# Statistics of the first two images from a separate 128-partition copy, and weights prepared in groups of three

## The reference

```python
xd = jnp.concatenate([x[:, :, 0::2, 0::2], x[:, :, 0::2, 1::2], x[:, :, 1::2, 0::2], x[:, :, 1::2, 1::2]], axis=1)
feats = jnp.concatenate([_dwconv(xd, w1, 1), _dwconv(xd, w3, 3), _dwconv(xd, w5, 5)], axis=1)
y = jnp.einsum('bchw,oc->bohw', feats, w_proj[:, :, 0, 0])
...
x = x + _L0_conv_ref(_gn(x), L0_conv_w1, L0_conv_w3, L0_conv_w5, L0_conv_w_proj)
```

## Time and profile before

| | us |
|---|---|
| median of three runs | 147.66 |
| lowest and highest | 146.65, 147.93 |
| the profiled execution | 147.7 |
| its span in the profile | 145.9 |
| TensorE busy (matmuls) | 129.1 |
| DVE busy | 119.8 |
| ACT busy | 103.0 |
| POOL busy | 98.3 |

### The profile page before, as it was taken

One profiled execution on the slowest core, in us unless ns is written; L12 is line 12 of the kernel. 1 busy time (PEld: TensorE's weight loads), 2 busy tenths in 40 slices (PEclk: granted clock), 3 DMA queues, 4 the chain that ended last, 5 costly groups with the idle time before them and its releaser, 6 DMA issues.

```text
span 145.9 us, 1480 instructions
## 1 busy us (share of the span) xinstructions
PE 129.1 (88%) x501; PEld 95.9 (66%) x501; DVE 119.8 (82%) x134; ACT 103.0 (71%) x110; POOL 98.3 (67%) x73
## 2 busy tenths in 40 slices
PE   0374699999999999999999999999999999999910
PEld 0222578788876777678767776777677867776600
DVE  0198999996299999999999999799938995999460
ACT  2285999999955999599959995999599950004100
POOL 7104799999699628994999399829993999100840
PEclk9999879999999999999999999999999999999996
DMA  3999993052043007000708699107094992853966
GB/s 101 216 210 212 209 211 50 0 110 49 0 98 57 0 19 136 0 4 17 136 0 180 122 186 206 38 17 136 0 216 84 174 198 55 180 112 85 196 145 150
DMA packets 35431, 15.73 MB, mean 108 GB/s; under 512 B 34016, under 2 KB 34144, under 8 KB 35040
## 3 DMA queue, kind: packets, MB, share of 16 engines
q1 hardware_dynamic: 33408, 8.39, 31.6%
q0 software_dynamic: 1440, 7.04, 24.9%
q10 hardware_dynamic: 576, 0.21, 0.6%
HBM read 4.41 MB, written 4.19 MB: 59 GB/s over the span
## 4 chain that ended last, share of the span: by engine, by line
PE 85%; DVE 4%; DMA 3%; ACT 2%; ACTq 1%; issue 1%; DVEq 1%; POOL 0%; POOLq 0%
PE YP L551 75%; PE YP L594 9%; DMA w_sb<-in_L_conv_w_dram 3%; DVE st L424 2%; DVE X L522 1%; ACT G L340 1%; DVE weff L449 1%; DVEq L86 0%; ACT HI L384 0%; PE SMALL L533 0%; POOL rstd L253 0%; ACTq L312 0%; ACTq L311 0%; PE SMALL L539 0%; ACTq L310 0%
## 5 line engine op out<-in xcount | busy, mean ns | idle before, releaser
L275 POOL TENSOR_TENSOR RING_SUM<-RING_SUM,PROD 128x900 f32<-128x900 f32 (+1 forms) x37 | 75.2, 2034 | 7.7 <-ACT PROD L365 3.8
L489 DVE SCALAR_TENSOR_TENSOR ACC<-G,coef,ACC 128x930 f32<-128x930 f32 (+1 forms) x64 | 76.6, 1197 | 2.0
L551 PE MATMUL YP<-HI,whi 128*128 128x512 f32 (+1 forms) x150 | 39.1, 413 | 2.8 <-ACT HI L384 2.8
L551 PE MATMUL YP<-LO,whi 128*128 128x512 f32 (+1 forms) x150 | 40.4, 420 | 0.0
L551 PE MATMUL YP<-HI,wlo 128*128 128x512 f32 (+1 forms) x150 | 37.7, 402 | 0.0
L551 PEld LDWEIGHTS YP<-HI,whi 128*128 128x128 f32 x150 | 29.5, 197 | 11.0 <-DVE whi L468 3.4
L365 ACT ACTIVATE PROD<-G,coef 128x900 f32<-128x900 f32 (+1 forms) x37 | 36.2, 1053 | 0.0
L551 PEld LDWEIGHTS YP<-LO,whi 128*128 128x128 f32 x150 | 28.5, 190 | 10.0 <-issue 3.4
L551 PEld LDWEIGHTS YP<-HI,wlo 128*128 128x128 f32 x150 | 28.3, 190 | 7.1
L375 ACT ACTIVATE Y<-YP 64x1024 f32<-64x1024 f32 x14 | 15.3, 1096 | 24.1 <-PE YP L594 23.9
L340 ACT ACTIVATE G<-X,nbias,rstd 64x1024 f32<-64x1024 f32 (+2 forms) x18 | 21.9, 1215 | 1.9 <-DVE nbias L442 1.5
(11 more groups left out here) (55 smaller groups left out, 50.3 us busy)
## 6 DMA issues: line engine op xcount, KB each, us to landing
LO<-G POOLq DMA_DIRECT2D x7, 543.0 KB, 4.9
X<-in_x_dram SPq DMA_DIRECT2D x12, 256.0 KB, 5.4
X<-Y POOLq DMA_DIRECT2D x3, 1024.0 KB, 7.0
out_dram<-X SPq DMA_DIRECT2D x12, 256.0 KB, 5.8
X<-in_x_dram SPq DMA_DIRECT2D x8, 128.0 KB, 4.3
out_dram<-X SPq DMA_DIRECT2D x8, 128.0 KB, 2.5
wp_sb<-in_L_conv_w_proj_dram ACTq DMA_DIRECT2D x1, 192.0 KB, 3.4
w_sb<-in_L_conv_w_dram ACTq DMA_DIRECT2D x1, 12.5 KB, 3.8
```

The lines of the kernel that those rows point to most:

```text
L275: pool.tensor_tensor(dst, dst, prod(b, k), ALU.add).then_inc(prod_added, 1)
L489: dve.scalar_tensor_tensor(part(ACC, tap), g_tap(b, tap), of5(tap), part(ACC, tap), ALU.mult, ALU.add).then_inc(acc_step, 1)
L551: mm = nc.tensor.matmul(dst, w[:, n, :], src, start=start, stop=False, skip_group_check=True)
```

## The change

- Images 0 and 1 get their statistics one by one. `load_parts` loads a second copy of each over all 128 partitions (a channel in four partitions, `XS`): image 0 in two DMAs ahead of everything else on SP's queue, image 1 behind image 0's normal load and w1. `part_bn` takes two statistics per image, spreads them with a mask, and a matmul with `same` (`sum_parts`) gives every partition the four parts of its channel; `part_variance` and `part_bias` finish it.
- The statistics of pairs 1 to 3 are as before but one place further on in `between`; `bn(1)` moves from ahead of the first tap into it.
- HI of image 0 is written straight from X: ACT writes three of four pieces (`high_half`), DVE one. G of image 0 is written after that, in one piece per column parity, and LO of image 0 as before from G and HI.
- The inner taps' weights come in three groups of three. ACT scales taps 0 to 4 and casts group 0; tap 5 is scaled behind ACT's first `high_half`; POOL scales taps 6 to 8. DVE casts groups 1 and 2. POOL subtracts group by group. The centre tap, which alone needs w1, becomes the last.
- The extra taps' scaling and cast move on ACT behind `products(0)`, and their `wlo` on POOL behind `sum_ring(0)`.
- w1 has its own load (SP's queue) and its own matmul. TensorE's `keep_warm` matmuls become 9 of 128 columns ahead of the transposes, 3 behind them, and 6 of 512 columns of zeros ahead of image 0.

```diff
-INNER = [(0, 0)] + [(dy, dx) for dy in (-1, 0, 1) for dx in (-1, 0, 1) if (dy, dx) != (0, 0)]
+INNER = [(0, -1), (0, 1)] + [(dy, dx) for dy in (-1, 1) for dx in (-1, 0, 1)] + [(0, 0)]
...
-WARM = (2, 2)
+WARM = (9, 3, 6)
+CHUNK = 3
+CHUNKS = N_INNER // CHUNK
+ACT_SCALED = 6
...
+            load_parts(sp, 0, 0, 512, xs_loaded[0])
+            load_parts(sp, 0, 512, 1024, xs_loaded[1])
+            load_image(sp, 0, image_loaded[0])
+            sp.dma_start(w_sb[:, W1_AT:N_COEF], w1.rearrange("c a h w -> c (a h w)")).then_inc(w1_loaded, 16)
+            load_parts(sp, 1, 0, 1024, xs_loaded[2])
+            load_image(sp, 1, image_loaded[1])
+            for b in range(2, B):
+                load_image(sp, b, x_loaded[b // 2])
...
+            pool.wait_ge(wpT_ready, 3)
+            pool.wait_ge(coef_copied, 1)
+            for n in range(ACT_SCALED, N_INNER):
+                pool.tensor_scalar(weff[:, n, :], wpT[:, 2, :], of5(PE_TAPS[n]), None, ALU.mult).then_inc(pool_scaled, 1)
             inv_std(1, 0, 1)
-
+            for k in range(CHUNKS):
+                taps = slice(k * CHUNK, (k + 1) * CHUNK)
+                pool.wait_ge(whi_ready, k + 1)
+                pool.tensor_tensor(wlo[:, taps, :], weff[:, taps, :],
+                                   whi[:, taps, :].bitcast(F32), ALU.subtract).then_inc(wlo_ready, 1)
+            inv_std(2, 1, 2)
+            sum_ring(0)
             pool.wait_ge(extra_ready, 1)
             pool.tensor_tensor(wlo[:, N_INNER:N_PE, :], weff[:, N_INNER:N_PE, :],
                                whi[:, N_INNER:N_PE, :].bitcast(F32), ALU.subtract).then_inc(extra_low_ready, 1)
-            pool.wait_ge(whi_ready, 1)
-            pool.tensor_tensor(wlo[:, 0:N_INNER, :], weff[:, 0:N_INNER, :],
-                               whi[:, 0:N_INNER, :].bitcast(F32), ALU.subtract).then_inc(wlo_ready, 1)
-            sum_ring(0)
-            inv_std(2, 1, 2)
+            inv_std(3, 2, 3)
...
             act.wait_ge(pads_zero, N_PADS)
+            act.wait_ge(image_loaded[0], 32)
             act.wait_ge(stats_ready, 1)
-
-            normalise(0, 0, TOP, g_top)
-            act.wait_ge(g_top, 2)
-            act.activation(s_image(HI, 0, 0, TOP), g_image(0, 0, TOP), ACT.Copy).then_inc(hi_top, 1)
-            normalise(0, TOP, PH, g_ready)
+            high_half(0, TOP, 0, hi_top)
+            scale_w5(5, ACT_SCALED)
+            high_half(TOP, PH, 0, hi_bottom)
+            high_half(TOP, PH, 1, hi_ready)
+            normalise(0, 0, PH, g_ready)
             act.wait_ge(g_ready, 2)
-            act.activation(s_image(HI, 0, TOP, PH), g_image(0, TOP, PH), ACT.Copy).then_inc(hi_ready, 1)
             products(0)
+            scale_w5(N_INNER, N_PE)
+            act.wait_ge(w5_scaled, ACT_SCALED + len(EXTRA))
+            act.activation(whi[:, N_INNER:N_PE, :], weff[:, N_INNER:N_PE, :], ACT.Copy).then_inc(extra_ready, 1)
...
+            def part_variance(b):
+
+                dve.wait_ge(spread_summed, b + 1)
+                dve.bn_aggr(agg1[:, b, :], SPREAD_PS[b]).then_inc(agg1_done, 1)
+                dve.wait_ge(agg1_done, b + 1)
+                dve.tensor_scalar(vare[:, b:b + 1], agg1[:, b, 1:2], EPS, None, ALU.add).then_inc(stat_step, 1)
...
-            between = {(0, 0): lambda: aggregate(1), (0, 2): lambda: (bn(2), aggregate(2)), (0, 3): lambda: variance(2, 1, 2),
...
+            between = {(0, 0): lambda: part_variance(1), (0, 1): lambda: (part_bias(1), bn(1)),
...
             for _ in range(WARM[1]):
-                keep_warm()
-            pe.wait_ge(whi_ready, 1)
+                keep_warm(ident[:, :], P)
+            pe.wait_ge(w_loaded, 32)
+            coefficients(0, W1_AT, coef_ready)
+            sum_parts(0)
```

More of the change, by code:

```diff
@@ L232, in _ @@
                                base=0, pattern=[[-1, P]], channel_multiplier=1).then_inc(const_step, 1)
+            pool.memset(same[:, :], 0.0).then_inc(stat_const, 1)
+            for k in range(PARTS):
+                pool.wait_ge(stat_const, k + 1)
+                v = same[:, :].rearrange("p (n c) -> p n c", c=C)
+                pool.affine_select(out=v, in_=v, compare_op=ALU.not_equal, fill=1.0, base=-k,
+                                   pattern=[[0, P // C], [-PARTS, C]], channel_multiplier=1).then_inc(stat_const, 1)
             a = avg[:, :].rearrange("p (b i c) -> p b i c", b=2, i=2)
@@ L319, in _ @@
                                ACT.Copy).then_inc(wpT_ready, 1)
+            act.wait_ge(coef_ready, 1)
+            act.activation(coef[:, 0:W1_AT], COEF_PS[:, 0:W1_AT], ACT.Copy).then_inc(coef_copied, 1)
             act.wait_ge(wpT_ready, 3)
@@ L326, in scale_w5, with high_half @@
                                    scale=of5(PE_TAPS[n])).then_inc(w5_scaled, 1)
-            scale_w5(0, N_PE)
-            act.wait_ge(w5_scaled, N_PE)
-            act.activation(whi[:, N_INNER:N_PE, :], weff[:, N_INNER:N_PE, :], ACT.Copy).then_inc(extra_ready, 1)
+            scale_w5(0, 5)
+            act.wait_ge(weff_step, CHUNK)
+            act.activation(whi[:, 0:CHUNK, :], weff[:, 0:CHUNK, :], ACT.Copy).then_inc(whi_ready, 1)
+            def high_half(r0, r1, j, done):
+                src = X[0:HALF, 0, r0:r1, :].rearrange("p h (w j) -> p h w j", j=2)[:, :, :, j]
+                act.activation(s_image(HI, 0, r0, r1)[HALF * j:HALF * (j + 1)], src, ACT.Identity,
+                               bias=nbias[0:HALF, 0:1], scale=rstd[0:HALF, 0:1]).then_inc(done, 1)
             def normalise(b, r0, r1, done):
@@ L452, in _ @@
+            part_bn(0)
             dve.wait_ge(wpT_ready, 3)
             dve.wait_ge(coef_copied, 1)
-            bn(0, 0, 2)
-            add_w3(0, 1, 2)
-            bn(0, 2, 4)
-            aggregate(0)
-            add_w3(3, 4)
-            variance(1, 0, 1)
-            add_w3(5, 6)
-            bias(1, 0, 1)
-            add_w3(7, 8)
-            dve.scalar_tensor_tensor(weff[:, 0, :], wpT[:, 0, :], coef[:, W1_AT:W1_AT + 1],
-                                     weff[:, 0, :], ALU.mult, ALU.add).then_inc(weff_step, 1)
@@ L471, in add_tap @@
+            cast_w(2)
+            part_bn(1)
             def add_tap(b, k):
@@ L525, in _, with keep_warm @@
         def _(pe):
-            pe.wait_ge(const_step, 4)
+            def keep_warm(tile, n):
+                nc.tensor.matmul(YP[:, 0, 0:n], tile, tile, start=True, stop=True)
+            pe.wait_ge(const_step, 3)
+            for _ in range(WARM[0]):
+                keep_warm(ident[:, :], P)
             for k in range(3):
```

203 lines of the change are left out of this document (137 added, 66 removed).

## The result

The changed kernel takes 149.64 us (median of four runs, 149.20 to 150.35) against 147.73 us: 1.0143 times as long, 95% interval 1.0104 to 1.0183. A few executions of some kernels take over 1.5% longer than the fastest of the same kernel; the ratios leave these out, the medians don't. The forecast was 148.3 us with a range of 146.5 to 150.0. The wait that it named is there, and the sum was 1.3 us low. The most useful finding came from the experiments, though: behind the wait that the forecast named stood a second one that it had missed, and with both gone the same change is 2.3 to 2.8% faster than the kernel before.

What follows compares the result with a forecast made beforehand. TensorE's row of matmuls behind a 16 us start was taken as the bound. From 147.7 us, 0.7 stays won of the 5.7 us earlier start and 1.3 is lost to the clock: 148.3 us, range 146.5 to 150.0.

Steps and rivals of the forecast that it cites:

- The wait that it named: TensorE ahead of image 0's extra taps, waiting for POOL's `wlo`: idle from S+17.3 to S+22.3, 5 us.
- What bounds the kernel: A start of 16 us, then TensorE's row of matmuls; the question is whether every later wait in its queue is met.
- S: Moment when the coefficients are copied and ACT begins to scale: 7.7 us before, 7.5 taken between 6.6 and 8.5.
- The third rival: Slower: matmuls ahead of the transposes hold the coefficients, S is 8.5, clock loss is whole: 150.0 us, chance 0.21.
- POOL's scaling: POOL scales three inner taps before image 0's root: 0.33 us each taken, bounds 0.29 and 0.56, under the variance's cover.
- HI by whi of image 0: TensorE's first matmuls of image 0: start at S+3.4, done at S+8.2, 12 matmuls after HI is complete at S+5.35.
- G of image 0: Written by ACT behind HI, complete at S+8.05; DVE's first tap waits for it.
- POOL, which decides: POOL's image 1 root by S+10.45, LO and four adds 10.7 us, `wlo` 0.99: extra taps at S+22.3, 29.8 us.
- The clock after the stall: TensorE's granted clock falls behind the 5 us stall, at the extra taps: 1.3 us lost, bounds 0 and 1.7.
- the forecast's own case: Wait for the extra taps' weights binds and clock is lost: 148.3 us, range 147.3 to 149.3, chance 0.57.
- the wait doesn't bind: Rival: POOL lets the extra taps' `wlo` out by S+17.3, so 142.0 us, some 143 with small waits; chance 0.09.
- What has no price: Items costed at nothing: XS loads, `part_bn(0)`, `bn(1)` behind the first tap, and the end, which moves with TensorE.

Runs made afterwards that it cites:

- run eight: Run six's kernel without the nine matmuls ahead of the transposes (zero instead of nine): 144.38 us, ratio 0.9870 to the kernel before.
- run eleven: Run six's kernel with POOL's border memsets behind DVE's copies of the projection and seven matmuls instead of nine ahead of the transposes: 143.56 us, ratio 0.9723.
- Run nine: Run six's kernel with POOL's inverse root of image 0 ahead of its three scalings instead of behind them: 143.91 us, ratio 0.9810.
- run six: Run one's kernel, with the averaging matmul of pairs 2 and 3 moved behind image 1's HI matmuls: 143.30 us; repeated for its profile, 143.47 us.
- Run five: Kernel before the change, with only POOL's rest of the extra taps' weights moved behind image 0's four adds: 147.64 us, ratio 1.0008.
- Run two: Changed kernel plus 16 matmuls of zeros on TensorE ahead of the wait for the extra taps' weights: 148.06 us, ratio 1.0052.
- run seven: Changed kernel with only the averaging matmul of pairs 2 and 3 moved behind image 1's HI matmuls: 149.41 us, ratio 1.0194.
- Run one: Changed kernel with POOL's rest of the extra taps' weights behind the first of image 0's four adds instead of the fourth: 149.41 us, ratio 1.0112.
- run four: Changed kernel with POOL's inverse root for image 1 behind image 0's LO, second run of it: 148.37 us, ratio 1.0087.
- ten: Run six's kernel with w1's load back on ACT's queue: median 145.64 us of six runs between 143.15 and 146.20, no ratio.

## Why the prediction was right, and where it wasn't

- **What bounds the kernel: right.** The forecast said that the start would gain about 5 us and that a later wait of TensorE decides. TensorE began image 0 4.5 us sooner and stood still 4.49 us (5 forecast), released by POOL's `wlo`.
- **When S comes: right in size, wrong in cause.** S was 7.64 us (7.5 taken). The nine matmuls took what was forecast (4.03 us; 3.9), but they ended 0.25 us ahead of the transposes, and run eight refutes them as the cause. The transposes waited for DVE's copies, and those for a projection that landed at 4.7 us and for POOL's memsets (run eleven). The clock did rise early: the six records behind the transposes took 0.83 us, where the 18 ahead of them had taken 0.22 each. The third rival, which rested on the matmuls, falls with the cause.
- **POOL's scaling: mis-sized.** 0.62 us each (1.85 us for three) against 0.33 taken and 0.56 as the upper bound. The root began 0.43 us behind its input. Run nine shows that nothing is to be had from it.
- **HI by whi of image 0: a wait missed.** It was to end 12 matmuls behind HI, at S+8.2; HI by wlo began at S+9.2. The third group's `whi` came only at 15.08 us, from DVE, for which the forecast has no term. In the changed kernel that vanishes in the stall; in run six's second profile it is the last thing that TensorE waits for.
- **G of image 0: right, but it decides nothing.** Complete at 15.92 us, S+8.3 (S+8.05 forecast). The first tap was to start there; DVE was free for it at 16.51, S+8.9, behind `part_bn(1)`, which the forecast doesn't price.
- **POOL, which decides: right.** From LO's start to the last add 18.84 to 29.47 us, 10.6 us (10.7 forecast). The extra taps at 30.48 us, S+22.8 instead of S+22.3: the tap's late start, 0.8 us, less 0.3 in the steps behind it. With S 0.14 late as well, nothing is left of the 0.7 us that were to stay. Run five shows that the place is harmless without the early start, as the forecast's reasoning demands.
- **The clock after the stall: right in kind, mis-sized.** 1.3 us was taken out of 0 to 1.7. It was 2.4 us in the profiled execution. The upper bound of 1.7 came from one occurrence, in which the clock was low from 16.8 to 20.2 us; here it was low from 29 to 36. Run two shows it alone: with the wait kept and the clock full, the 36 matmuls take 2.4 us less. But run seven's profile has the same stall and 1.5 us, so the term has no one size.
- **The sum: two terms missed.** 147.7 - 0.7 + 1.3 became 147.7 + 0 + 2.4 in the profiled execution of 150.06 us, and 1.9 more than before in the medians.
- **Two slips in the working.** The third rival's text gives POOL's slow scaling 0.5 us and its sum adds 0.3; with 0.5 it comes to 31.3 and 150.2 us. And by the prices per record the steps of the early clock, 5.1, 5.5 and 6.1 us, are the ends of the nine matmuls, the transposes and the three matmuls, one step ahead of those that they are set beside; S = 6.6 stands.
- **The range: partly luck.** 149.64 lies above the 147.3 to 149.3 of the forecast's own case and nearest to the 150.0 of the third rival, whose cause run eight refutes. And the kernel is slower clear of noise (1.0 to 1.8%), to which 0.26 was given, against 0.63 for a change within 1%.
- **The sentence that failed outright** is the rival "the wait doesn't bind: 142.0, some 143". Run one made it so, and the time was 149.4. The forecast set out to ask whether every later wait in TensorE's queue is met, and didn't look at the matmul that averages the statistics of pairs 2 and 3. Two rows of the kernel before show its slack of 6 us:

```profile
32.74 0.26 DVE L428 BATCH_NORM_AGGREGATE agg<-st 128x2 f32<-128x24 f32 x1
...
38.98 0.28 PE L539 MATMUL WT_PS<-agg,avg 128*128 128x4 f32 x2
```

  The change puts the aggregation behind F (at 37.28 us in run one), which takes 4.5 us of that slack, and an early TensorE takes the rest. The 142 to 143 us are what both waits out give (143.3 and 143.5).
- **What has no price: half right.** No F held TensorE in the changed kernel's profile, and of the loads only w1's, 0.81 us ahead of the matmuls of zeros. The late `aggregate(3)` and `part_bn(1)` were left out of that list.

## What to carry to other kernels

When one engine's queue is the bound, go through every wait in that queue and write down its slack; a change that makes the engine early by more than the smallest slack meets that wait, and taking out only the first can show nothing. An experiment that removes the named wait and leaves the time as it was doesn't refute the wait: look for the next one. And count an idle stretch of TensorE for more than its length: here 4.5 us of it cost 1.5 us more in one execution and 2.4 in another, and filling it with matmuls of zeros won back 1.3 us by the ratios.

## What the runs showed of the hardware that wasn't expected

A small DVE instruction can be held for as long as POOL's running instruction takes. `spread` took 0.21 us, and 2.33 us beside POOL's LO (run four); in the changed kernel the bias of image 1 took 2.10 us beside the same instruction:

```profile
19.18 2.10 DVE L502 SCALAR_TENSOR_TENSOR nbias<-agg,rstd 128x1 f32<-128x1 f32 x1
```

One of DVE's copies took over 1 us beside POOL's memsets, and all three took 0.5 us once these were moved away (run eleven), which is the one place where it was tested.

It can also come out differently in two executions of one kernel. With both waits out, the second of DVE's three steps for the variance of pairs 2 and 3 took 0.16 us in an execution of 143.76 us and 1.86 us in one of 146.63 us:

```profile
39.64 0.16 DVE L519 TENSOR_TENSOR dev<-dev 128x2 f32<-128x2 f32 x1
```

```profile
40.60 1.86 DVE L519 TENSOR_TENSOR dev<-dev 128x2 f32<-128x2 f32 x1
```

The traces show what differs: where the step lies against POOL's adds. In the first, the step began 0.2 us before POOL's last add of image 1 (39.86 us), while the add ahead of it was ending. In the second it began 0.1 us after that add (40.51) and ended as the add ended, at 42.46 us. The profiles of runs eight, ten and eleven agree: 0.25 us before the add, 0.16 us; 0.1 us after it, 1.87 and 1.85 us. In all three profiles with the long step, TensorE later idled 1.1 us ahead of ring(1) for DVE's F of image 1; in the two with the short one it didn't. So a few tenths of a microsecond in the order of two engines go with a wait of 1.1 us in TensorE's row. That this step alone makes the difference in time wasn't tried.

What is held has something in common. `spread`, the bias and this step read two tensors in SBUF. The first and third of the three steps and DVE's taps from the second on have one of their two inputs in PSUM (`WT_PS`, `ACC`), and took 0.16 and 1.2 us beside the same adds. The Trainium skill, page "GPSIMD Engine Reference", section "Specifications", says that the SBUF interfaces are shared with VectorE, with contention for VectorE's instructions in a two-port mode and those with two SBUF inputs. The trace agrees for the two-input steps; whether the copies ran in a two-port mode it doesn't show. How long the hold lasts the runs show themselves: to the end of the POOL instruction, 1.85 to 2.33 us here.
